# Which query tile of each head goes through DVE and DRAM: the sixth in place of the fifth, one step later

## What is computed

```python
qkv = xn @ qkv_w + qkv_b                                   # 16 heads of 128
scores = einsum('bhid,bhjd->bhij', q, k) + alibi_mask      # causal: j <= i only
attn = softmax(scores, axis=-1)
ctx = einsum('bhij,bhjd->bhid', attn, v)
out = ctx @ out_w + out_b
h = silu(xn @ lut[gate_idx].T) * (xn @ lut[up_idx].T)      # 688 wide, LUT of 16
ffn = h @ lut[down_idx].T
```

## Time and profile before

| | |
|---|---|
| median of three runs | 517.88 us (517.37 to 518.29) |
| the profiled execution | 519.0 us, of which the span from first to last instruction 517.2 us |
| busy time: TensorE, DVE, ScalarE, GpSimd | 506.4, 414.9, 320.1, 340.6 us |
| transposes on TensorE (line 570) | 496 |
| block transposes (line 956), stores, loads back | 16, 64, 16 |

### The profile page before, as it was taken

The page is one execution under the profiler, slowest core; times in us unless marked ns, Lnnn a source line. Parts: engine busy times, 40 slices in busy tenths (PEclk is TensorE's granted clock), DMA queues, the critical chain, the costliest instruction groups (busy, mean ns, idle before and its releaser), DMA issues. The chain is left out here.

```text
span 517.2 us, 10365 instructions
## 1 busy us (share of the span) xinstructions
PE 506.4 (98%) x3142; PEld 455.1 (88%) x3142; DVE 414.9 (80%) x1044; ACT 320.1 (62%) x656; POOL 340.6 (66%) x372
## 2 busy tenths in 40 slices
PE   7998999999999999999999999999999998999997
PEld 6786989989899889988998989988998897998897
DVE  6698797889788988989798978898898978764451
ACT  4786665767575756576675756585657656664430
POOL 3446776688767965787578876796678567962300
PEclk9998999999999999999999999999999999999999
DMA  7942030203011110203020302021011101010001
GB/s 267 133 87 67 0 94 1 73 21 91 0 54 37 46 46 4 69 19 91 0 71 20 91 0 67 24 48 43 28 43 27 46 14 38 3 52 1 0 22 61
DMA packets 19846, 24.56 MB, mean 47 GB/s; under 512 B 2288, under 2 KB 13552, under 8 KB 19696
## 3 DMA queue, kind: packets, MB, share of 16 engines
q1 hardware_dynamic: 18784, 23.24, 14.7%
q0 software_dynamic: 1040, 1.05, 2.4%
HBM read 17.99 MB, written 6.29 MB: 47 GB/s over the span
## 5 line engine op out<-in xcount | busy, mean ns | idle before, releaser
L1111 POOL TENSOR_TENSOR w_ffn<-w_ffn,term 128x1088 f32<-128x1088 f32 x60 | 152.7, 2545 | 73.7 <-DVE term L934 73.7
L719 ACT ACTIVATE work<-work,neg_max 128x128 f32<-128x128 f32 (+7 forms) x128 | 98.8, 772 | 34.6 <-DVE neg_max L919 34.6
L919 DVE CUSTOM_DVE_ANT_0 work<-ps_s,alibi 128x128 f32<-128x128 f32 (+7 forms) x128 | 96.0, 751 | 5.4 <-issue 4.9
L947 DVE TENSOR_TENSOR p_t_lo<-ps_t,p_t_hi 128x512 fp32r<-128x512 f32 (+3 forms) x160 | 85.5, 559 | 15.6 <-ACT p_t_hi L726 15.5
L1089 POOL TENSOR_SCALAR work<-work,inv_sum 128x128 f32<-128x128 f32 (+7 forms) x128 | 95.8, 748 | 0.0
L726 ACT ACTIVATE p_t_hi<-ps_t 128x512 fp32r<-128x512 f32 (+3 forms) x160 | 74.1, 496 | 26.2 <-PE ps_t L570 26.1
L570 PE MATMUL ps_t<-ident,work 128*128 128x128 f32 x496 | 73.6, 275 | 1.7 <-DVE p_t_lo L947 1.6
L448 PE MATMUL ps_u<-p_t_hi,v_hi 128*128 128x512 f32 x192 | 66.5, 346 | 2.3 <-DVE p_t_lo L962 1.9
L702 ACT ACTIVATE qk_hi<-ps_u,bias_now 128x512 fp32r<-128x512 f32 x64 | 44.2, 691 | 37.9 <-PE ps_u L450 37.8
L448 PE MATMUL ps_s<-qk_hi 128*128 128x128 f32 (+2 forms) x192 | 67.2, 350 | 0.5 <-DVE qk_lo L895 0.5
L450 PE MATMUL ps_u<-p_t_hi,v_lo 128*128 128x512 f32 x192 | 66.9, 349 | 0.0
(11 more groups left out here) (123 smaller groups left out, 1187.3 us busy)
## 6 DMA issues: line engine op xcount, KB each, us to landing
scratch<-blocks SPq DMA_DIRECT2D x64, 80.0 KB, 2.3
raw<-scratch SPq DMA_DIRECT2D x16, 320.0 KB, 2.9
qk_raw<-w_qk SPq DMA_DIRECT2D x16, 256.0 KB, 2.8
w_ffn<-idx SPq DMA_DIRECT2D x1, 2176.0 KB, 10.7
v_raw<-w_v SPq DMA_DIRECT2D x8, 256.0 KB, 2.7
o_raw<-w_o SPq DMA_DIRECT2D x8, 256.0 KB, 3.0
acc<-b_out POOLq DMA_DIRECT2D x1, 1024.0 KB, 18.1
out<-acc SPq DMA_DIRECT2D x8, 128.0 KB, 1.7
```

What stands on the lines that cost most here:

```text
L719: act.activation(slot(i), slot(i), ACT.Exp, bias=neg_max[:, col:col + 1], scale=-1.0, accum_out=row_sum[:, col:col + 1]).then_inc(exp_done, 1)
L919: dve.tensor_tensor_reduce(slot(i).rearrange("p (b c) -> p b c", b=banks), made_of, alibi[:, p, S - width:S].rearrange("p (b c) -> p b c", ...
L947: dve.tensor_tensor(p_rows(1, i, g), ps_t[:, room, 0:len(turned(i, g)) * P].rearrange("p (j q) -> p j q", q=P), p_rows(0, i, g).bitcast(F3 ...
L1111: pool.tensor_tensor(piece, piece, term[:, :], ALU.add).then_inc(term_added, 1)
```

## The change

PLACED goes from 4 to 5: the sixth tile, 768 wide instead of 640, is turned in 32x32 blocks by DVE and placed through DRAM, and the fifth is turned by TensorE, in step 7. BLOCKS_AT goes from 6 to 7, since the sixth tile is normalised a step later. The buffers `raw`, `blocks` and `scratch` grow by a fifth with BAND. `placed_rows` takes the columns of the sixth tile, and `mask` waits for DVE's own block transpose where slot 1 is written again (tile 1) and not slot 0. The turn of tile 5 in step 0 of the next head and in the tail falls away on TensorE, ScalarE (line 726) and DVE (line 947).

```diff
--- before.py
+++ after.py
@@ -48,7 +48,7 @@
 SUM_AT = 1, 2, 4, 7
 FFN_LO_AT = {3: 0, 4: 1, 6: 2, 7: 3}
 LAG = 3
-BLOCKS_AT = 6
+BLOCKS_AT = 7
 PLACED_HI_AT = 2
 PLACED_LO_AT = 2
 
@@ -56,7 +56,7 @@
 
 B32 = 32
 BANDS = P // B32
-PLACED = 4
+PLACED = 5
 BAND = (PLACED + 1) * B32
 GROUPS = [-(-(i + 1) // 4) if i != PLACED else 0 for i in range(NT)]
 GROUPS_BEFORE = [sum(GROUPS[:i]) for i in range(NT + 1)]
@@ -291,7 +291,7 @@
         def placed_rows(part):
 
             rows = p_t[part][:, 0:(PLACED + 1) * PT_ROW].rearrange("p (j q) -> p j q", q=PT_ROW)
-            return rows[:, :, 0:P].rearrange("p j (a c) -> p j a c", c=B32)
+            return rows[:, :, (PLACED - 4) * P:(PLACED - 3) * P].rearrange("p j (a c) -> p j a c", c=B32)
 
         def head_no(n, p):
 
@@ -908,7 +908,7 @@
                     dve.wait_ge(made, 4)
                 elif i == 0:
                     dve.wait_ge(alibi_ready, 2 * n + p)
-                if i == 0 and not (kind == FIRST and p == 0):
+                if i == PLACED - 4 and not (kind == FIRST and p == 0):
                     dve.wait_ge(blocks_turned, head_no(n, p))
                 elif i >= 4 or not (kind == FIRST and p == 0):
                     dve.wait_ge(p_turned, groups_to(n, p, i - 4))
```

## The result

The changed kernel took 531.41 us in the median of 4 runs (530.47 to 533.46), the kernel before 518.09 us of 4 (517.37 to 518.45): ratio 1.0264, 95% interval 1.0230 to 1.0298. The forecast was 533.7 us, slower, with a range of 524 to 541. The profiled execution took 532.01 us with a span of 530.2, so 13.0 us more than the profiled one of before, by time and by span.

The account below looks back on a forecast made before the run. TensorE was taken to bound the kernel, with 0.58 us of slack at each head boundary. Loop 10.0, head 1 1.1, heads 14 and 15 0.3, tail 2.8, clock 1.6: 15.8 us more, so 533.7 us, range 524 to 541.

Parts of the forecast that it names:

- The boundary: Between two loop heads: ctx_t_lo frees pv0's PSUM bank late, so TensorE's second projection waits 0.7 us per head.
- The saved transpose: TensorE turns 30 tiles per head instead of 31, worth 0.10 us a head, 1.6 us over 16 heads.
- place_lo and the DMA: Loop heads: place_lo's undisturbed part grows 0.13 us, which counts; the load back takes 0.2 us more, free.
- rival E: DMA is late: blocks land over 1 us later, ScalarE stands at place_hi; 6 us on top, 540; chance 0.06.
- The look-up: DVE, step 7: starting later it meets less of GpSimd's work, near 0.85 us instead of 1.36, shedding 0.5.
- Rival C: Small stall: DVE or the look-up quicker than set, 0.3 us per head, no clock loss; 525 us; chance 0.10.
- A: The forecast itself: ctx_t_lo late at each boundary, the load late in the tail; 526 to 540 us, chance 0.67.
- Head 1: Has v3 where loop heads have the projections, no slack before: 1.1 us, bounds 0.7 and 1.3.
- Heads 14 and 15: One unit at the boundary and waits of their own that swallow the lateness: 0.3 us together.
- The tail: After the last head the load back comes late, delaying p_lo(6) and TensorE's transposes of tile 7: 2.8 us.
- a fall of the clock: Tail: its idle, longer than one that preceded a granted clock of 0.50, costs 1.6 us, bounds 0 and 1.6.

Follow-up runs that it names:

- blocks_behind: Changed kernel with DVE's block transpose of tile 5 moved behind the units' lo steps in step 7; 529.62 us, ratio 1.0238.
- idle_512: Kernel before with an idle DVE transpose of 512 columns ahead of step 7's look-up, nothing moved; 517.76 us, ratio 1.0006.
- loop_and_tail2: Changed kernel with step 7's look-up behind the units in heads 0 to 13 and the tail's placed tile after tile 7's turn; 520.38 us.
- tail_late: Changed kernel with the tail's placed tile taken after the turn of tile 7; 530.15 us, ratio 1.0234.
- step7_alone: Kernel before with only BLOCKS_AT 7 in place of 6, tile 4 still the placed one; 518.88 us, ratio 1.0017.
- loop_only2: Changed kernel with step 7's look-up behind the units in heads 0 to 13 only, tail unchanged; 522.74 us, ratio 1.0100.
- lookup_behind: Changed kernel with step 7's look-up moved behind the units' lo steps in every head; 529.49 us, ratio 1.0206.

## Why the prediction was right, and where its terms were off

**The boundary: right, in kind and size.** The prediction had a slack of 0.58 us, additions of 1.71 us on DVE and a look-up 0.5 us cheaper, so that ctx_t_lo should end 1.0 to 1.2 us later and TensorE wait 0.7 us at the second projection. ctx_t_lo ends 2.40 us behind scores(0)'s start (before 1.81), which is itself 0.58 later in its head: 1.17 us. The 12 heads grew by 9.72 us, forecast 10.0; 0.81 us each instead of 0.83. The bracket shows only 0.52 and 0.39 us as waiting, since it counts from the modelled end of the last matmul. From start to start, the matmul ahead of the wait takes 0.91 us (239.71 to 240.62) and its neighbours 0.23: 0.68 us are lost. blocks_behind, which has no such wait, says the same: from scores(0) to scores(1) it takes 3.21 us in every loop head, the changed kernel 3.95 and 3.82 in turn, 0.67 us more on average.

**The saved transpose: 0.10 us a head forecast, nothing measured.** Without the six transposes of tile 5, scores(0) to scores(1) take 3.21 us in blocks_behind, before 3.77: 0.56 less. With the five of tile 4, scores(7) to the next scores(0) take 3.81 and 3.78 us, before 3.24 and 3.22: 0.57 and 0.56 more. One transpose fewer thus gave no time in any loop head. A head's 0.81 us are 0.67 for the wait, 0.13 for place_lo and 0.01 for this.

**place_lo and the DMA: sizes right.** place_lo went from 1733 to 1870 ns at the median and the transpose from 834 to 969 (forecast +0.13, 0.97). That place_lo's growth counts, and at the transposes of tile 1, is what the rows of step 4 show. The load was given 0.2 us more and took none. place_hi never waited in the loop; rival E falls with that.

**The look-up, 0.85 forecast, 0.89 measured.** Had it stayed at 1.36, the loop would have cost more. Rival C hangs on a still quicker one. Its terms, 3.6 + 1.6 + 1.4 + 2.5, are 9.1 and give 527 us, not the 525 written there; so C's time lay inside A's range, and what speaks against it is the wait of 0.67 us a head, not the total.

**Head 1: undersized.** 1.1 forecast (0.7 to 1.3), 1.5 measured. TensorE waits 1.81 us there for ctx_t_lo, ahead of a unit of values. The forecast carried the loop's sum over, in a head whose waits no row had shown.

**Heads 14 and 15: wrong sign.** +0.3 forecast, -1.0 measured. Head 14 is 0.7 us shorter. Its wait of 0.47 us ahead of tile 7's transposes is gone in the changed kernel, and no wait for ctx_t_lo came in its place. The forecast had these heads' own waits swallow a loss, and didn't ask whether the change would take such a wait away.

**The tail: mechanism right, clock wrong.** 2.8 forecast, 2.2 measured, with ScalarE's idle of 3.40 us for the load (forecast 4) and TensorE's wait of 2.16 (forecast over 2). The 1.6 us for a fall of the clock behind it didn't come: PEclk stayed 1.00 over 474 to 484 us. That term is the step that failed. Against the profiled 13.0 us the forecast's 15.8 was 2.8 too high: 1.6 by the clock, 1.3 by heads 14 and 15, 0.6 by the tail's wait, 0.3 by the loop; head 1 (0.4) and the start (0.5) stood on the other side. That the total came as near as it did is in part luck: the forecast was too low by 0.9 us in head 1 and at the start, and that took off a quarter of what it had too much elsewhere.

**What the 1.6 us were worth.** A fall costs that much, but it isn't tied to the length of an idle. idle_512 and the kernel before have the same head 1 with the same idle (1.96 and 1.95 us): it took 26.31 us without a fall and 27.88 with one, 1.57 us. The times of idle_512 come in two groups, seven from 517.4 to 517.8 at a mean clock of 0.999 or 1.000 and five from 519.05 to 519.31 at 0.997. So it was a chance per execution, and should have been priced as one: at about half of 1.6, and for the kernel before as well. Between executions without a fall the change costs 13.2 us (530.47 and 530.81, against a mean of 517.44 over nine of before, 516.98 to 517.79).

**The start.** 0.5 us of the profiled difference stood before anything that the change touches; in loop_and_tail2's profiled execution it was 3.5 us (first scores(0) at 20.94 instead of 17.40). No single profile should be subtracted from another without looking at its first 20 us.

## What to carry to other kernels

When an engine's operation frees a buffer for the bottleneck, the time between its end and that use is the budget for everything put ahead of it in that queue. Here 1.2 us of added work made the release 1.14 us late and cost 0.67 us a pass. Added work isn't lateness, though: 0.6 us of it was free, since the look-up behind it got shorter by nearly as much. Ahead of moving work off the bottleneck, list what is queued between it and the next release, and put what nobody waits for (here the look-up, 0.84 us) behind the release. Where a look-up feeds another engine's in-order queue, check what stands behind it there: the same move was worth 8 us in the loop and lost as much in the last two heads and the tail. And a wait of 0.1 us in each pass shows in no bracket; it shows when the same stretch of the bottleneck is measured from start to start in both kernels.

## What the runs showed of the hardware

The granted clock fell or not behind the same idle. In loop_and_tail2's timeline and table by stretches, the wait that left the clock at 1.00 in the changed kernel (2.08 us) is followed by 0.51:

```profile
51.47 0.47 PE L448 MATMUL ps_u<-p_t_hi,v_hi 128*128 128x512 f32 x1 [2.08 <-DVE p_t_lo L962]
...
52.00:54.00 2.00, 2.00 (x6) 0.51 0.00 0
```

Idles of 1.81, 1.95, 2.08 and 2.67 us were followed by a fall in one execution, idles of 1.81, 1.96, 2.00, 2.08, 2.16 and 2.45 in another by none; behind 3.27, 4.09 and 4.90 it fell each time. The Trainium skill, TensorE: Matmul & The Clock Gate, section "What's actually happening", says that one kernel can meet the gate differently from run to run; the times of idle_512 agree.

The four stores of the last head landed, by the issue of the load behind them, after 3.2 to 3.5 us in five executions (the changed kernel, tail_late, step7_alone, loop_only2, loop_and_tail2), after 5.12 in lookup_behind and 4.25 in blocks_behind. No run tells why.
